# Layer 1's key mask: added by GpSimd from a row loaded for each pair, in place of products on TensorE

## The reference

```python
    xn = _ln(x, ln_w, ln_b)
    q = xn @ Wq + bq
    k = xn @ Wk + bk + (1.0 - src_mask) * -1000000.0
    q = jax.nn.softmax(q.reshape(b, t, h, dh), axis=-1)
    k = jax.nn.softmax(k.reshape(b, t, h, dh), axis=1)
    v = ((xn @ Wv + bv) * src_mask).reshape(b, t, h, dh)
    att = jnp.einsum('bnhd,bnhl->bhdl', k, v)
    y = jnp.einsum('bnhd,bhdl->bnhl', q, att).reshape(b, t, d)
    emb_out = (jax.nn.silu(emb) @ W_emb + b_emb)[:, None, :]
    scale, shift = jnp.split(emb_out, 2, axis=2)
    hh = _ln(y, ln2_w, ln2_b) * (1.0 + scale) + shift
    hh = jax.nn.silu(hh) @ W_out + b_out
    return x + hh
```

## Time and profile before

| | us |
|---|---|
| median of 3 runs | 1095.91 (1095.82 to 1096.64) |
| the profiled execution, its own time | 1097.78 |
| its span from first to last instruction | 1096.0 |
| TensorE busy in the span | 1054.8 (96%) |
| VectorE busy | 759.8 (69%) |
| ScalarE busy | 591.6 (54%) |
| GpSimd busy | 448.6 (41%) |
| mean granted TensorE clock | 0.993 |

### The profile page before, as it was taken

The page is one execution under the profiler, slowest core; times in us unless marked ns, Lnnn a source line. Parts: engine busy times, 40 slices in busy tenths (PEclk is TensorE's granted clock), DMA queues, the critical chain, the costliest instruction groups (busy, mean ns, idle before and its releaser), DMA issues. The chain is left out here.

```text
span 1096.0 us, 25953 instructions
## 1 busy us (share of the span) xinstructions
PE 1054.8 (96%) x8696; PEld 909.8 (83%) x8696; DVE 759.8 (69%) x1326; ACT 591.6 (54%) x1960; POOL 448.6 (41%) x783
## 2 busy tenths in 40 slices
PE   6999999999999999999999999999999999999995
PEld 4878888888888888888887778888888888888884
DVE  4656766676666766667678787777777777777764
ACT  5366667776677766776588443433343443434431
POOL 3242434334343343433343344444444444444432
PEclk9999999999999999999999999999999999999997
DMA  8824110111101111011102211111111111111011
GB/s 275 256 84 141 42 61 24 62 62 41 60 24 62 62 41 59 25 62 63 43 23 98 95 50 33 40 55 57 57 57 57 57 57 57 52 52 39 31 38 58
DMA packets 46017, 71.65 MB, mean 65 GB/s; under 512 B 10256, under 2 KB 14448, under 8 KB 45968
## 3 DMA queue, kind: packets, MB, share of 16 engines
q1 hardware_dynamic: 45968, 71.02, 20.3%
HBM read 54.19 MB, written 16.79 MB: 65 GB/s over the span
## 5 line engine op out<-in xcount | busy, mean ns | idle before, releaser
L1276 PE MATMUL bank<-xt_hi,w_hi 128*128 128x256 f32 x768 | 228.4, 297 | 3.1 <-DVE xt_lo L893 3.1
L1277 PE MATMUL bank<-xt_lo,w_hi 128*128 128x256 f32 x768 | 218.5, 284 | 0.0
L1278 PE MATMUL bank<-xt_hi,w_lo 128*128 128x256 f32 x768 | 218.3, 284 | 0.0
L454 POOL TENSOR_SCALAR stat<-stat 128x1 f32<-128x1 f32 x128 | 34.5, 270 | 441.8 <-DVE stat L884 417.7
L613 ACT ACTIVATE prob<-prob,neg_max 128x128 f32<-128x128 f32 x512 | 198.7, 396 | 6.7 <-DVE neg_max L907 6.6
L632 ACT ACTIVATE th<-z_s 128x512 f32<-128x512 f32 x64 | 40.5, 633 | 249.9 <-POOL z_s L488 249.8
L1276 PE MATMUL bank<-w_hi,xt_hi 128*128 128x512 f32 x384 | 158.3, 412 | 1.0 <-DVE w_lo L835 1.0
L1276 PEld LDWEIGHTS bank<-xt_hi,w_hi 128*128 128x128 f32 x768 | 148.9, 194 | 9.1 <-DVE w_lo L835 4.8
L1278 PE MATMUL bank<-w_hi,xt_lo 128*128 128x512 f32 x384 | 150.5, 392 | 0.0
L1277 PE MATMUL bank<-w_lo,xt_hi 128*128 128x512 f32 x384 | 149.8, 390 | 0.0
L1277 PEld LDWEIGHTS bank<-xt_lo,w_hi 128*128 128x128 f32 x768 | 148.6, 193 | 0.0
(11 more groups left out here) (130 smaller groups left out, 2203.3 us busy)
## 6 DMA issues: line engine op xcount, KB each, us to landing
x_in<-in_x_dram SPq DMA_DIRECT2D x32, 256.0 KB, 2.8
x_res<-in_x_dram SPq DMA_DIRECT2D x32, 256.0 KB, 2.9
between_layers<-x_res SPq DMA_DIRECT2D x32, 256.0 KB, 2.0
x_in<-between_layers SPq DMA_DIRECT2D x32, 256.0 KB, 2.8
x_res<-between_layers SPq DMA_DIRECT2D x32, 256.0 KB, 2.8
out_dram<-x_res SPq DMA_DIRECT2D x32, 256.0 KB, 2.6
room<-in_L_cond_W_emb_dram SPq DMA_DIRECT2D x8, 512.0 KB, 7.3
prob<-in_L_cond_emb_w_dram SPq DMA_DIRECT2D x4, 512.0 KB, 7.5
```

Source lines behind the costliest of these rows:

```text
L454: pool.tensor_scalar(v[:, 8:9], v[:, 7:8], EPS, None, ALU.add).then_inc(s[a_in].sem, 1)
L1276: pe.matmul(o, a_hi, b_hi, start=start, stop=False)
L1277: pe.matmul(o, a_hi, b_lo, start=False, stop=False)
L1278: return pe.matmul(o, a_lo, b_hi, start=False, stop=stop)
```

## The change

The three parts, `mask_wide`, `ones_parts` and the products with them go. Layer 1's mask bias is stored as float32 in a second DRAM tensor; for each pair SyncE loads the pair's 256 values, broadcast to all partitions, into `mask_pair` (`load_mask_pair`). GpSimd adds it to the keys in `q_t` behind each `k_out` (`mask_keys`, once per block), and `k_soft` on VectorE waits for that instead of for `k_out`. On ScalarE `qt_out` 1 moves ahead of the exps of block 0. Two waits move to step 0 so that the tiles from which the masks are stored aren't overwritten early.

```diff
+            def load_mask_pair(f):
+                sp.wait_ge(*done(s["kmask1"], f + (-GROUP)))
+                at = f + (-B)
+                flat = mask_bias[1].rearrange("(o b) p -> o (b p)", o=1)
+                row = (flat[:, at.const * P:at.const * P + N] if at.reg is None
+                       else flat[:, bass.ds(at.value() * P, N)])
+                sp.dma_start(mask_pair[:], row.broadcast_to([P, N])).then_inc(s["mask_pair_in"].sem, 16)
...
                 if k:
                     load_back(1, k, 1)
+                if n:
+                    load_mask_pair(n)
+                if k:
                     store(1, k, 0)
...
+            def mask_keys(f, slot, pair):
+                if pair == 0:
+                    pool.wait_ge(s["mask_pair_in"].sem, (f + (-B)).value() * (16 // GROUP) + 16)
+                pool.wait_ge(*done(s["ka_out" if pair == 0 else "kb_out"], f))
+                kv = k_exp[:, slot, pair * D:(pair + 1) * D].rearrange("p (j n) -> p j n", j=2)
+                pool.tensor_tensor(kv, kv, mask_pair[:].rearrange("p (o n) -> p o n", o=1).broadcast_to([P, 2, N]), ALU.add
+                                   ).then_inc(s[f"kmask{pair}"].sem, GROUP)
...
-                pool.memset(mask_wide[:], 0.0).then_inc(wide_clear, 1)
...
                 residual(0, k, 0)
+                if i == G - 1:
+                    mask_keys(f, slot, 0)
+                    mask_keys(f, slot, 1)
                 norm1(n, 1)
                 norm2(k, 0)
...
+                if f:
+                    mask_keys(f, slot, 0)
                 if k:
                     residual(1, k, 0)
+                if f:
+                    mask_keys(f, slot, 1)
+                if k:
                     norm2(k, 0)
                 if n:
                     norm1(n, 1)
...
                     k_out(1, f, slot, 0)
+                if k:
+                    qt_out(k, 1)
+                if f:
                     k_exps(f, slot, 0)
-                if k:
-                    qt_out(k, 1)
-                if f:
                     k_out(1, f, slot, 1)
                     k_exps(f, slot, 1)
...
             def k_soft(f, slot, pair):
-                dve.wait_ge(*done(s["ka_out" if pair == 0 else "kb_out"], f))
+                dve.wait_ge(*done(s[f"kmask{pair}"], f))
...
-                    if l == 1:
-                        at = f + (-B)
-                        cols = (mask_wide[:, at.const * P:at.const * P + N] if at.reg is None
-                                else mask_wide[:, bass.ds(at.value() * P, N)])
-                        pe.matmul(o, ones_parts[:], cols, start=True, stop=False)
                     for kc in range(C):
                         last = three(o, hi[l][w][:, kc, c * P:(c + 1) * P], lo[l][w][:, kc, c * P:(c + 1) * P],
-                                     xt_hi[:, slot, kc, :], xt_lo[:, slot, kc, :], kc == 0 and l == 0, kc == C - 1)
+                                     xt_hi[:, slot, kc, :], xt_lo[:, slot, kc, :], kc == 0, kc == C - 1)
```

More of the change, by code:

```diff
@@ L16 @@
 MASKED = -1000000.0
-PART_ROWS = (0, 32, 64)
 class At:
@@ L79, in build @@
     WQ, WK, WV, WO = range(4)
-    mask_bias = nc.dram_tensor("mask_bias", [B, P], F32, kind="Internal").ap()
+    mask_bias = [nc.dram_tensor(f"mask_bias{l}", [B, P], F32, kind="Internal").ap() for l in range(2)]
     middle = nc.dram_tensor("between_layers", [B, T, D], F32, kind="Internal").ap()
@@ L196, in build @@
         cond_in, cond_act, cond_pe, cond_dve = (sem(f"cond_{n}") for n in ("in", "act", "pe", "dve"))
-        mask_in, mask_cut, mask_saved, mask_moved, mask_pe, mask_ready = (
-            sem(f"mask_{n}") for n in ("in", "cut", "saved", "moved", "pe", "ready"))
+        mask_in, mask_cut, mask_saved, mask_pe, mask_ready = (
+            sem(f"mask_{n}") for n in ("in", "cut", "saved", "pe", "ready"))
         norm_in = [sem(f"norm_in{l}") for l in range(2)]
@@ L226, in build @@
                     "exp0 exp1 exp2 exp3 rec pt_pe0 pt_pe1 pt_pe2 pt_pe3 pt_out0 pt_out1 pt_out2 pt_out3 pv_out")
-        s |= stages("kt_pe kt_out qt_out att_out kmax0 kmax1 kexp0 kexp1 krec q_pe q_add qmax qsub qexp qsum qrec", B)
+        s |= stages("kt_pe kt_out qt_out att_out kmask0 kmask1 kmax0 kmax1 kexp0 kexp1 krec q_pe q_add qmax qsub qexp qsum qrec", B)
         for n in ("x_in_full", "res_in", "stored", "mask_row_in"):
             s[n] = [Stage(sem(f"{n}{b}")) for b in range(GROUP)]
+        s["mask_pair_in"] = Stage(sem("mask_pair_in"), B)
         src = [t["x"], middle]
@@ L321, in load_mask @@
                 at = f + b
-                row = mask_bias[at.const:at.const + 1, :] if at.reg is None else mask_bias[bass.ds(at.value(), 1), :]
+                row = mask_bias[0][at.const:at.const + 1, :] if at.reg is None else mask_bias[0][bass.ds(at.value(), 1), :]
                 sp.dma_start(mask_row[:, b, :], row.broadcast_to([P, P])).then_inc(s["mask_row_in"][b].sem, 16)
+            def load_mask_pair(f):
[5 more added lines that the diff above has]
+                sp.dma_start(mask_pair[:], row.broadcast_to([P, N])).then_inc(s["mask_pair_in"].sem, 16)
             def load_back(l, k, b):
@@ L365, in start @@
                 load_wide(1, WO, OUT_BIAS[1])
[L366 to L370, removed]
+                sp.wait_ge(mask_cut, 4)
+                sp.dma_start(mask_bias[1], mask_tmp[1][:, P:2 * P]).then_inc(mask_saved, 16)
                 sp.wait_ge(bias_sum_pe, 3)
@@ L396, in step0 @@
                 if i == G - 2:
+                    sp.wait_ge(mask_saved, 32)
+                    load_mask_pair(n)
                     sp.wait_ge(bias_pe, TURN[1, WK])
@@ L441, in _ @@
             pool.memset(ones_32nd[:], 1.0 / 32).then_inc(once, 1)
[L442 to L447, removed]
+            pool.wait_ge(once, 4)
             pool.tensor_tensor(pick[:], ident[:, 0:2 * B], ident[:, 2 * B:4 * B], ALU.add).then_inc(consts, 1)
@@ L720, in step0 @@
                 y_t_out(k, 1)
+                if i == 0:
+                    act.wait_ge(mask_saved, 32)
                 tanh(k, 0)
@@ L776, in step1 @@
                 if f:
+                    k_exps(f, slot, 0)
                     k_out(1, f, slot, 1)
```

23 lines of the change are left out of this document (3 added, 20 removed).

## The result

| | before | after |
|---|---|---|
| median of 5 runs, us | 1096.64 (1095.82 to 1097.82) | 1128.30 (1127.07 to 1128.76) |
| profiled execution, own time / span | 1097.78 / 1096.0 | 1128.76 / 1126.9 |
| TensorE busy in the span | 1054.8 (96%) | 1057.0 (94%) |
| VectorE / ScalarE / GpSimd busy | 759.8 / 591.6 / 448.6 | 750.5 / 590.9 / 484.5 |
| mean granted clock | 0.993 | 0.992 |

The kernel is slower: the ratio is 1.0284 (95% interval 1.027 to 1.0298). GpSimd is busy 35.9 us more, the time lost is 31.7 us; that the two are close is chance, as the experiments show.

What follows compares the result with a forecast made beforehand. TensorE was taken to bound layer 1 at 29.90 us a step, the ring taking the same time. 13 x 2.25 = 29.3, less 0.3, gave +29.0: 1126.8 us profiled, 1124.9 as median; range 1111 to 1142.

Steps and rivals of the forecast that it cites:

- The ring: Layer 1's loop from x's moments over norms, tanh, sum and store to the next x: from 29.90 to 32.15 us.
- rival of hidden masks: In layer 1 the loop has over 2 us of unseen slack, TensorE stays the bound: 1091.1 us, chance 0.10.
- dear masks: GpSimd's masks collide with VectorE's two-operand instructions, or new waits cost its sequencer: 1136 to 1146 us, chance 0.15.
- falling clock: TensorE's new waits ahead of the turned y halve its clock in each step: 1167 us, chance 0.04.
- The chain's length: From x's moments over first mask, k_max, exps, k_out and second mask, the norm of y starts 2.25 us late.
- The step: Steps 17 to 29 of layer 1, 13 of them, each grow by 2.25 us from 29.90 to 32.15.
- the 0.39 us ahead of the second norm: GpSimd's time there: hidden under new waits, 1113.5 us; 0.39 more for each of two new waits, 1146.
- Where TensorE waits: TensorE waits 2.55 us per step, mostly ahead of the turned y, a few tenths ahead of query(k, 1) and output products.
- mixed step: There the masks come behind both k_out and ahead of k_max, which VectorE reaches late anyway: zero.
- step 16: First step of layer 1: k_max was late already because an output product lies between the key blocks: zero.
- Step 30: No x is normalized there, the first mask starts right behind k_out and both fit: gains 0.30 us.
- The removed products: 64 mask products on TensorE, four per pair of sequences: 0.30 us per step, 4.8 us over 32 pairs.

Runs made afterwards that it cites:

- e3: The change with both mask additions still made on GpSimd, but into a tile nobody reads, and k_max waiting for k_out alone: 1104.61 us.
- e2: The change with the loads of the mask's row kept and the additions dropped, k_max waiting for k_out alone: 1093.03 us.
- e5: The change with the first mask moved ahead of the first norm of x on GpSimd in layer 1's steps: 1097.31 us.
- e10: The change with only the second norm of x moved behind the first z_s on GpSimd, its moments behind VectorE's first scaling of z: 1113.07 us.
- e1: The change with qt_out 1 put back behind the first exps on ScalarE, as before the change: 1136.86 us.
- e4: The change with the second k_out ahead of the first exps on ScalarE: 1111.67 us.
- e12: e4 with one needless reduction more on VectorE, right ahead of the subtraction of the queries' maximum: 1104.91 us.
- e7: The change with the mask added by VectorE ahead of each k_max instead of by GpSimd: 1111.31 us.
- e11: e9 with the first load of the mask's row made one step earlier: 1094.84 us.
- e9: e5 with the second norm of x also moved behind the first z_s on GpSimd, its moments behind VectorE's first scaling of z: 1095.53 us.

## Why the prediction was right, step by step

The forecast was +29.0 us; between the medians it was +31.7, and between the two spans +30.9.

- **The ring** is what happened, and it was shown in four ways. Additions that nobody waits for cost a quarter (e3); the loads cost nothing in the loop (e2); a mask moved out of the chain gives back everything (e5); and a norm of x that has nothing to do with masks, taken out of the ring, gives back 15 us (e10). The rival of hidden masks falls with the result, the dear masks with the next point, the falling clock with 1.00 in the ten steps (e1, with waits 0.2 us longer, has it).
- **The chain's length.** Forecast 2.25 us late at the norm of y; in the step shown 9.14 less 6.83, 2.31. Each of its terms held: 1.28 and 1.27 for the masks (1.29 forecast), 0.72 from k_max to exp, 1.56 for the exps, 0.95 from the second k_out to the second mask (0.99). The records of the mask, over the whole kernel (count, min/median/max in ns):

```profile
L493 POOL TENSOR_TENSOR q_t<-q_t,mask_pair x32: 1261/1271/1298, 591.8 to 1080.0; 128x512 f32<-128x512 f32 x32
```

- **The step** grew by 2.38 us instead of 2.25: 12 steps make 28.6, and step 17 grew by 1.49 (30.04 to 31.53), perhaps because the ring only begins to close there. Together 30.1, against 29.3 forecast for the 13. So 0.13 us per step was missing from the term, and that it came so near is partly luck. In the step shown, handovers 0.06 us longer (mask to k_max, mask to norm) make the chain 2.31. But the rows followed the longer of the loop's two steps. In the other, the norm of y began 6.32 us after x's moments (804.77 to 811.09) and now begins 9.34 after them (817.07 to 826.41), 3.02 later. GpSimd's rows, before and after:

```profile
811.09 0.23 POOL L454 TENSOR_SCALAR stat<-stat 128x1 f32<-128x1 f32 x1 [1.74 <-DVE stat L884]
...
826.41 0.23 POOL L457 TENSOR_SCALAR stat<-stat 128x1 f32<-128x1 f32 x1
```

Over eleven rounds of the ring (from the moments at 684.91 before, at 687.65 after) the way from x's moments to the norm of y grew from 6.55 to 9.24 us in the mean, 2.69 and not 2.25. The way from there to z_s shrank from 7.65 to 7.44, and the rest of the round from 15.69 to 15.63. So the term was 0.44 us too small, and the pieces taken as fixed gave back 0.27. Part of that is the 0.39 us ahead of the second norm: by the earlier trace rows it was a wait for VectorE's moments, not a price of GpSimd's sequencer as the rival of the dear masks had it, and behind the later norm of y it is gone. Nor is the other step as far below 29.90 as this one is above it, as the prediction says: its round was 29.59 us, against 30.38.

- **Where TensorE waits** came as told: 1.75 us in each step for yn, a few tenths for s_lo and ahead of the second query, about 2.4 in all (24.8 us in 340) where the sum has 2.55.
- **The term that was wrong** is the mixed step, counted at zero. The argument there was on k_max; the load of the mask, the first on a busy queue ahead of x, was looked at only inside the loop. It cost 1.31 us at the start of step 16, of which 0.23 was there ahead of step 14 already. The prediction's own sign for it (x's moments waiting longer for their DMA) is what showed it.
- **Step 30** was to gain 0.30 and gained 0.07 (28.93 to 28.86); step 16 gained 0.34 where nothing was expected, the tail 0.13. These cancel to 0.24 us and were not traced.
- **The removed products** were worth 0.38 us per step by e2, 0.30 by the sum. In steps 17 to 29 the change could not gain from it, since the ring set their length.

So the sum was 2.7 us short of the medians' difference: about 1.1 from the load, 0.8 from the ring's size, and the rest from small terms and from profiled executions that differ by a microsecond from their medians.

## What to carry to other kernels

Where one engine is full, look for a second loop through the step (here from a load over moments, norms, tanh, the sum and the store to the next load) and compare its length with the step before moving work to an idle engine: GpSimd was 41% busy and had no room where it mattered, and room of 8 us one place earlier in its program. Put the new work ahead of what it would hold up, where the engine waits anyway; the same two additions cost 31 us in one order and nothing in the other. And count the new loads at every place of the program, the one outside the loop too.

## What the hardware showed that was not expected

Adding 0.7 us of work on VectorE per step made a kernel 6.8 us faster (e4 to e12), because it changed which of two colliding instructions began first. In the rows shown, where z_s began first it lasted 1.05 us and VectorE's subtraction 1.32 to 1.42; where z_s began second it lasted 1.49 and the subtraction 0.93. The Trainium skill says so (SBUF — State Buffer, section "Who interferes with whom": "Issue order, not op shape, decides who blocks"), and the traces agree: the one that began second was held up most. As the first of the two VectorE's subtraction paid a little too: it lasts 0.69 us in the change, where the two do not overlap. The prediction used that page for the lengths of the masks, where nothing collided; it did not ask whether a shift of a few tenths in the ring turns such a pair round elsewhere, and that is where the expectations of e3, e4 and e7 went wrong, as far as e12 and the rows show.

The other thing is TensorE's clock. Between bursts of work at a granted clock of 1.00, a single wait of TensorE of about 2 us was followed by a stretch at 0.50 in six of ten cases in e1, and once each in e10 and e11, but not in e9 behind a like wait. None of the change's waits for yn between 690 and 1070 us, up to 1.84 us long, was. Whether the length of the wait decides it was not tried.
